# Dropping the padding of the stored head rows, and sharing out the last unit and the last layout

## The reference

```python
h = tok(x) ; h = concat([cls, h])                       # 128 x 17 x 256
h = h + attn(layernorm(h), wq, wk_a, wk_b, wv_a, wv_b, wo)
y = layernorm(h)
dist = softmax(mean(y @ Wr + br, axis=1))               # over 16 heads
idx = sort(top_k(dist, 4))                              # 4 heads of each image
Q, K, V = (y @ W + b, split into heads, gathered by idx, for W in Wq, Wk, Wv)
O = softmax(Q @ K.T / 8) @ V                            # 128 x 4 x 17 x 64
h = h + (O laid side by side, 17 x 256) @ Wo + bo
```

## Time and profile before

| | |
|---|---|
| runs | 415.77 us median of 3 (414.05 to 419.84) |
| the profiled execution | 419.29 us, span 417.0 us |
| mean granted TensorE clock | 0.844 of full speed |
| busy | PE 327.1 us (78%), PEld 264.0, DVE 253.6 (61%), ACT 200.6 (48%), POOL 170.6 (41%) |
| packets of the DMA queues | q1 (SP) 46944, q10 (ACT) 928, q0 (GpSimd) 576 |

### The profile page before, as it was taken

How to read it: one execution, slowest core, us unless ns; L and a number is a source line. 1 busy time by engine, 2 the same in 40 slices (tenths; PEclk the granted TensorE clock), 3 DMA queues, 4 the chain that set the end, 5 groups by cost and what they waited for, 6 DMA issues and landing times. The chain is left out here.

```text
span 417.0 us, 15363 instructions
## 1 busy us (share of the span) xinstructions
PE 327.1 (78%) x6575; PEld 264.0 (63%) x6575; DVE 253.6 (61%) x539; ACT 200.6 (48%) x453; POOL 170.6 (41%) x190
## 2 busy tenths in 40 slices
PE   1999999888977787757972588887978978562877
PEld 1896666435755566546851588877977877562466
DVE  2454354534678888875967387777766666441165
ACT  1113342544887766723890357666645656330240
POOL 3862000003366666630550824556673466424300
PEclk9999999999975555556995589999989999875889
DMA  7999000004400000000000779778787877822604
GB/s 214 398 422 404 29 2 0 0 0 153 151 5 4 6 6 3 5 3 4 2 1 0 232 221 301 225 225 221 216 247 222 244 208 217 243 46 60 211 27 191
DMA packets 48516, 55.98 MB, mean 134 GB/s; under 512 B 21536, under 2 KB 45248, under 8 KB 47936
## 3 DMA queue, kind: packets, MB, share of 16 engines
q1 hardware_dynamic: 46944, 52.54, 39.7%
q0 software_dynamic: 576, 2.23, 1.7%
q10 hardware_dynamic: 928, 0.23, 0.2%
HBM read 45.02 MB, written 9.96 MB: 132 GB/s over the span
## 5 line engine op out<-in xcount | busy, mean ns | idle before, releaser
L478 POOL TENSOR_TENSOR r<-r,cst 128x1088 f32<-128x1088 f32 x16 | 33.0, 2068 | 68.3 <-DVE ring L874 65.5
L1243 PE MATMUL ps<-r 128*128 128x256 f32 x192 | 46.1, 397 | 8.7 <-DMA r<-in_x 8.7
L1243 PEld LDWEIGHTS ps<-r 128*128 128x128 f32 x192 | 38.1, 201 | 17.5 <-issue 12.3
L1348 PE MATMUL ps<-r 17*32 17x34 f32 x2048 | 30.3, 242 | 17.2 <-DVE r L937 12.6
L1348 PEld LDWEIGHTS ps<-r 17*32 17x32 f32 x2048 | 27.1, 141 | 25.1 <-DVE r L937 19.5
L670 ACT ACTIVATE r<-r,cst 128x136 f32<-128x136 f32 x128 | 39.9, 399 | 0.0
L561 POOL TENSOR_TENSOR r<-r,quad 128x476 f16<-128x476 f16 x40 | 39.0, 1008 | 0.0
L1462 PE MATMUL ps<-r,ring 128*128 128x68 f16 x840 | 38.4, 203 | 0.0
L1460 PE MATMUL ps<-tile_head,wb 128*128 128x68 f16 x140 | 28.1, 201 | 12.8 <-DMA ring<-wsplit 11.1
L740 ACT ACTIVATE r<-ps 128x504 f16<-128x504 f32 (+1 forms) x50 | 32.0, 667 | 11.4 <-PE ps L1440 10.8
L1440 PE MATMUL ps<-pairs_of,r 128*128 128x56 f16 x680 | 30.4, 195 | 8.9 <-DVE r L1109 5.6
(11 more groups left out here) (158 smaller groups left out, 756.6 us busy)
## 6 DMA issues: line engine op xcount, KB each, us to landing
ring<-wsplit SPq DMA_DIRECT2D x140, 192.0 KB, 3.3
r<-in_x SPq DMA_DIRECT2D x3, 1536.0 KB, 15.8
padded_rows<-r SPq DMA_DIRECT2D x38, 112.0 KB, 3.0
r<-in_w SPq DMA_DIRECT2D x4, 768.0 KB, 12.1
wsplit<-ring SPq DMA_DIRECT2D x1, 3072.0 KB, 11.7
r<-in_x SPq DMA_DIRECT2D x4, 384.0 KB, 8.5
h<-in_pos SPq DMA_DIRECT2D x1, 1536.0 KB, 11.9
out<-h SPq DMA_DIRECT2D x3, 512.0 KB, 3.2
```

The lines of the kernel that those rows point to most:

```text
L478: pool.tensor_tensor(free(kx[:, u % 2, 0, :], (ROWH, UI), (NTOK, HH), (1, NTOK)), free(kr[:, 0, UI * NTOK * u:], (NTOK, UI), (0, HH), (1, ...
L1243: mm = pe.matmul(bank((n - 1) % 2, 0, D), xT[:, c, k, i * P:(i + 1) * P], tokw[:, k, :], start=k == 0, stop=k == PKT - 1)
L1348: mm = pe.matmul(bank(4 + 2 * (u % 2) + j // 2, at, at + 2 * NTOK)[QROW * c:QROW * c + QROW], v1[rows, UG * u + g, lo:lo + QROW], p1T[rows ...
```

## The change

Six things are altered. (1) `padded_rows` has a pitch of 17 rows a pair instead of 32, and each store takes 17 rows instead of 32. (2) The last unit is stored in halves: two times two transfers of seven tiles by SP and as many by ACT. (3) Of the last unit's block-diagonal matrices POOL makes those of half 0 and ACT those of half 1, in eight instructions of its own (one for each of four pairs, times two parts). (4) The product of the last half has PSUM bank 4, so it doesn't wait for DVE, and TensorE runs nine of the keep-awake matmuls before the last unit's products. DVE takes the last unit's score maxima before the second `head_out` of the unit before. (5) At the end POOL lays out slot 2 and the larger part of slot 3, DVE slot 0 and the first part of slot 3, ACT slot 1. (6) The ten turns go in the order `TURN_ORDER`, in which both halves alternate.

```diff
-PITCH = QROW * HD2
+PITCH = NTOK * HD2
...
-        def pair_rows_of(v, j):
-            return bass.AP(padded_rows.tensor, (v * PU + j) * PITCH, [(HD2, QROW), (IPG * PITCH, GU), (1, HD2)])
+        def pair_rows_of(v, j, lo=0, n=GU):
+            return bass.AP(padded_rows.tensor, (v * PU + IPG * lo + j) * PITCH,
+                           [(HD2, NTOK), (IPG * PITCH, n), (1, HD2)])
+        def stores(i):
+            return 16 * IPG * (len(range(i, NV, 2)) + (i == (NV - 1) % 2))
+        def weigh_bank(v, r):
+            return 4 if (v, r) == (NV - 1, 1) else 7
...
+        TURN_ORDER = [(0, 0), (0, 1), (1, 0), (0, 2), (1, 1), (0, 3), (1, 2), (0, 4), (1, 3), (1, 4)]
+        def laid_out(s, part):
+            lo, hi = (OG_FIRST, NTOK) if part else (0, OG_FIRST)
+            return (free(og2[:, lo, HD2 * s:], (D, hi - lo), (1, HD2)),
+                    free(og[:, s, HD2 * lo:], (HD2, hi - lo), (1, HD2)))
...
             def store_pairs(v, j):
-                sp.dma_start(pair_rows_of(v, j), o2[QROW * j:QROW * j + QROW, v % 2])\
+                sp.dma_start(pair_rows_of(v, j), o2[QROW * j:QROW * j + NTOK, v % 2])\
                     .then_inc(o2_stored[v % 2], 16)
...
-            for v in range(NV - 3, NV):
+            for v in range(NV - 3, NV - 1):
                 sp.wait_ge(o2_ready, 2 * (v + 1))
-                for j in range(IPG if v < NV - 1 else IPG // 2):
+                for j in range(IPG):
                     store_pairs(v, j)
+            for r in range(2):
+                sp.wait_ge(o2_ready, 2 * (NV - 1) + r + 1)
+                for j in range(IPG // 2):
+                    sp.dma_start(pair_rows_of(NV - 1, j, GR * r, GR),
+                                 o2[QROW * j:QROW * j + NTOK, (NV - 1) % 2, GR * r:GR * r + GR])\
+                        .then_inc(o2_stored[(NV - 1) % 2], 16)
...
-                    for r in range(2):
+                    for r in range(2 if v < NV else 1):
                         for x in range(2):
                             block_diagonal(v - 1, r, x)
...
+            for s, part in ((2, 0), (2, 1), (3, 1)):
+                pool.wait_ge(og_ready[s], 16)
+                dst, src = laid_out(s, part)
+                pool.tensor_copy(dst, src).then_inc(og2_pool, 1)
...
+            for x in range(2):
+                act.wait_ge(pT_low if x else pT_high, NV)
+                if x == 0:
+                    act.wait_ge(pv2_done, 2 * (NV - 2))
+                for i in range(IPG):
+                    nc.scalar.activation(free(bd[:, (NV - 1) % 2, x, GR, QROW * i:], (P, GR), (1, NTOK)),
+                                         free(p2Tx[:, (NV - 1) % 2, x, GR], (QROW, GR), (1, NTOK)), ACT.Copy,
+                                         scale=quad[:, i:i + 1]).then_inc(bd_last, 1)
...
-            dve.tensor_scalar(idx[:, :], at_slot, float(QROW), None, ALU.mult).then_inc(idx_ready, 1)
+            dve.tensor_scalar(idx[:, :], at_slot, float(NTOK), None, ALU.mult).then_inc(idx_ready, 1)
...
             def weigh2(v, r):
-                pe.wait_ge(bd_ready, 4 * v + 2 * r + 2)
+                last = (v, r) == (NV - 1, 1)
+                if last:
+                    pe.wait_ge(bd_last, 2 * IPG)
+                else:
+                    pe.wait_ge(bd_ready, 4 * v + 2 * r + 2)
...
-                if 2 * v + r >= 1:
+                if 2 * v + r >= 1 and not last:
                     pe.wait_ge(o2_ready, 2 * v + r)
...
+            keep_awake(9)
             weigh2(NV - 1, 0)
             weigh2(NV - 1, 1)
...
-            for i in range(len(BATCHES)):
-                turn_heads(0, i)
+            turn_heads(0, 0)
+            turn_heads(0, 1)
             turn_heads(1, 0)
             for i, batch in enumerate(BATCHES):
+                if i + 2 < len(BATCHES):
+                    turn_heads(0, i + 2)
                 if i + 1 < len(BATCHES):
                     turn_heads(1, i + 1)
```

More of the change, by code:

```diff
@@ L78, in build @@
     with ExitStack() as ctx:
-        padded_rows = nc.dram_tensor("padded_rows", (NPAIR * QROW, HD2), F32, kind="Internal").ap()
+        padded_rows = nc.dram_tensor("padded_rows", (NPAIR * NTOK, HD2), F32, kind="Internal").ap()
         wsplit = nc.dram_tensor("wsplit", (NE, P, WHEAD), F16, kind="Internal").ap()
@@ L204, in build @@
         bd_ready = sem("bd_ready")
+        bd_last = sem("bd_last")
         ps_clear = sem("ps_clear")
@@ L336, in turn_bank @@
         def turn_bank(k, i):
-            return i % 2 if k else i
+            return TURN_ORDER.index((k, i)) % 2
         def turned_heads(k, i, x):
@@ L580, in _ @@
             for i in range(2):
-                pool.wait_ge(o2_stored[i], len(range(i, NV, 2)) * IPG * 16)
+                pool.wait_ge(o2_stored[i], stores(i))
             pool.wait_ge(idx_ready, 1)
@@ L814, in _ @@
                                  scale=WS).then_inc(wo2_high, 1)
[L815 to L835, removed]
+            for r in range(2):
+                act.wait_ge(o2_ready, 2 * (NV - 1) + r + 1)
+                for j in range(IPG // 2, IPG):
+                    act.dma_start(pair_rows_of(NV - 1, j, GR * r, GR),
+                                  o2[QROW * j:QROW * j + NTOK, (NV - 1) % 2, GR * r:GR * r + GR])\
+                        .then_inc(o2_stored[(NV - 1) % 2], 16)
+            act.wait_ge(og_ready[1], 16)
+            for part in range(2):
+                dst, src = laid_out(1, part)
+                nc.scalar.activation(dst, src, ACT.Copy).then_inc(og2_act, 1)
+            for e, (k, i) in enumerate(TURN_ORDER):
+                act.wait_ge(og_turned, e + 1)
+                if k == 1 and i >= 2:
+                    act.wait_ge(wo2_done, BATCHES[i - 2][-1] + 1)
+                n = P * len(BATCHES[i])
+                nc.scalar.activation(turned_heads(k, i, 0), bank(turn_bank(k, i), 0, n), ACT.Copy, scale=XS)\
+                    .then_inc(ogT_high, 1)
         @block.vector
@@ L1201, in _, with lay_out @@
                                      op1=ALU.subtract).then_inc(wo2_split, 1)
-            def lay_out(s):
+            def lay_out(s, part):
                 dve.wait_ge(og_ready[s], 16)
-                for lo, hi in ((0, OG_FIRST), (OG_FIRST, NTOK)):
-                    dve.tensor_copy(free(og2[:, lo, HD2 * s:], (D, hi - lo), (1, HD2)),
-                                    free(og[:, s, HD2 * lo:], (HD2, hi - lo), (1, HD2))).then_inc(og2_dve, 1)
+                dst, src = laid_out(s, part)
+                dve.tensor_copy(dst, src).then_inc(og2_dve, 1)
             def low_heads(k, i):
-                e = len(BATCHES) * k + i
+                e = TURN_ORDER.index((k, i))
                 dve.wait_ge(ogT_high, e + 1)
@@ L1214, in low_heads @@
                     .then_inc(ogT_ready, 1)
-            lay_out(0)
+            lay_out(0, 0)
+            lay_out(0, 1)
             low_heads(0, 0)
+            lay_out(3, 0)
             low_heads(0, 1)
-            lay_out(2)
-            for i in range(2, len(BATCHES)):
-                low_heads(0, i)
             low_heads(1, 0)
             for i, batch in enumerate(BATCHES):
+                if i + 2 < len(BATCHES):
+                    low_heads(0, i + 2)
                 if i + 1 < len(BATCHES):
@@ L1508, in weigh2 @@
                     for m, (b, x) in enumerate(((0, 0), (0, 1), (1, 0))):
[L1509 removed]
+                        mm = pe.matmul(bank(weigh_bank(v, r), HD2 * i, HD2 * i + HD2), bd[:, v % 2, b, g, :], v2[:, v % 2, x, g, :],
                                        start=m == 0, stop=m == 2)
@@ L1545, in turn_heads @@
             def turn_heads(k, i):
[L1547 to L1550, removed]
-                    pe.wait_ge(ogT_ready, i + 1 if i < 2 else e - 1)
+                if k == 0:
+                    pe.wait_ge(og2_dve, 1 if i == 0 else 2)
+                    pe.wait_ge(og2_act, 1 if i == 0 else 2)
+                else:
+                    pe.wait_ge(og2_dve, 3)
+                    pe.wait_ge(og2_pool, 1 if i == 0 else 3)
+                e = TURN_ORDER.index((k, i))
+                if e >= 2:
+                    pe.wait_ge(ogT_ready, e - 1)
                 for at, n in enumerate(BATCHES[i]):
```

11 lines of the change are left out of this document (7 added, 4 removed).

## The result

The changed kernel takes 503.81 us (median of 4 runs, 503.39 to 504.37), the kernel before 414.91 (413.61 to 419.84): ratio 1.2125, 95% interval 1.207 to 1.218. The profiled execution took 504.23 us for a span of 502.4, 85.4 more than the profiled one of before, which lay above its median. Some executions of the kernel before are over 1.5% above its fastest; the medians behind the experiments, and the ratios, leave such executions out.

What follows compares the result with a forecast made beforehand. It took the one DMA engine receiving all 17-row stores as the bound: 267.1 + 50.4 weights + 173.3 stores + 1.6 + 5 = 497.4, plus 31.1 tail gives span 528.5, time 530.8, less 3.5: 527 us; range 480 to 600.

Steps and rivals of the forecast that it cites:

- One engine a store: Stores of 17 rows: each goes to one DMA engine, the same each time; stores land 111.5 us later; 75 in 100.
- even spread: Rival for 17-row stores: uneven shares over nine or more engines, so no change or small gain, 411 us; 12 in 100.
- engines in turn: Rival for 17-row stores: one engine each, but a different one in turn, 412 to 430, say 418 us; 5 in 100.
- the one with gaps: Rival for one-engine stores: each transfer starts only when the one before has ended, +70 us, 597 us; 7 in 100.
- The price of a piece: Stores: each 256 B piece takes 18.2 ns on its engine, so 9520 pieces take 173.3 us.
- the floor of 10.1 ns: Low bound on a 256 B store piece, from the rate of long loads: -77 us, 450 us; inside the forecast.
- the row at 20.5: High alternative for a 256 B store piece, 20.5 ns with two queues at once: +22 us, 549 us; inside the forecast.
- Does the engine ever run dry: Stage two's loop: SP's queue always has next entries, so the engine never idles; remaining weight loads add 50.4 us.
- The 3.5 us taken off at the end: Whole kernel: the earlier profiled execution lay 3.5 us above its median, so the forecast was lowered from 530.8 to 527 us.
- The signs: Changed profile: one completion packet a store, units of about 25 us, weight waits over 100 us, last stores near 497.
- The last unit: Last unit's edits: products ready by 463 under the store backlog, so worth nothing; without the backlog 2 to 3 us.
- The tail: After the last store: new layout copies and turn order change 0, bounds -1.5 and +2; 31.1 us stay.

Runs made afterwards that it cites:

- the 16 + 1 split: Changed kernel with each store cut into rows 0 to 15 per pair plus one transfer for row 16 of all four pairs: 414.4 us, ratio 1.000.

## Why the prediction was right, and which terms were off

**One engine a store: right.** The count of completion packets in the earlier trace rows gave two readings, equal shares or uneven ones; 17, 18, 19 and 25 rows on 1, 9, 1 and 5 engines, and 16 and 4 rows on 16 and 4, are what the rule of the divisor says. The Trainium skill's page "DMA: Bandwidth & Descriptors", section "Why a DMA increments its semaphore by 16 and not by 1", states this rule, and the trace agrees in all these counts. That it is the same engine each time is shown by the stores of one unit, which follow each other at 3.33 us instead of running side by side, and by the two queues that together move 18 GB/s. So the rivals of an even spread and of engines in turn fell, and the one with gaps fell too: the 18 GB/s go on from store to store.

**The price of a piece: too high.** I took 18.2 ns from the share of DMA time in the earlier trace rows. Durations overlap: the one engine starts a piece each 14.0 ns. Over 9520 pieces that is 133.3 instead of 173.3 us, -40. It was the largest miss, and the floor of 10.1 ns and the row at 20.5 lay on both sides.

**"Does the engine ever run dry": it does.** The prediction had SP running ahead, so that work other than stores cost 50.4 us, with 6.6 for start, landing and small packets; 5 of these 6.6 had no row behind them. From the first store at 267.71 to 470.34 are 202.6 us, less 133.3 are 69.3: +12.3 on those 57.0. By the packets the engine takes no store for 65.1 us between the first block of stores and the last, instead of the 50.4, while start and landing together are 3.1 and not 6.6; the pieces come to 1.2 more than at 14.0 ns. The step forgot that the issuing queue has only so much room. With one engine behind it SP is held at each store, issues the weights late, and then a register load of 1.4 to 3.1 us in each unit is in the open. Moving it gave 13.3 us back. With the first store 0.6 later the sum is 497.4 - 40.0 + 12.3 + 0.6 = 470.3, as measured.

**The 3.5 us taken off at the end: wrong here.** They stood for the distance of the profiled execution of before from its median. The four executions of the changed kernel lie within 1.0 us, the profiled one 0.4 above the median. So of the 23 us between 527 and 503.81 the pieces and the weights explain 27 down, and the tail, the end of the execution and this correction some 3.5 up. Two misses of opposite sign met, which is luck in part: with the price of a piece right and everything else as predicted the forecast would have been 487, near the lower end of its range.

**The signs: most came.** Completion packets were one a store, the units took 23.7 us on average for the 25 forecast, and one long wait came in each unit. The waits for weights over 100 us did not come: they were 67.6. The last three units have no weights behind their stores, and their delay shows as the 25.7 us at the end.

**The last unit: right.** The products were done at about 444.6, 25.7 us before the stores landed, so its edits were worth nothing here; the prediction had the products by 463 and the engine held by older stores till 480. Without the backlog they are worth 2.2 to 2.6 us by medians and 3.0 in the profile, for the 2 to 3 forecast.

**The tail: right within its bounds.** 32.1 instead of 31.1 us in the changed kernel, 0.4 in medians between the two tails on short stores: it is no gain. The stretch itself varies with the granted clock, whichever tail it has: the old tail took 29.1 us at 0.90 behind the 17-row stores alone and 31.1 at 0.88 before, the new one 29.1 at 0.90 in the kernel with the register load moved and 32.1 at 0.81 in the changed one.

**The even-spread rival's size.** It was put at 411 with the last unit's edits. The nearest thing measured is the 18-row store with nine equal shares and the same edits, 408.6 and 410.3 on two chips.

## What to carry to other kernels

Before cutting rows off a transfer, look at what the number of rows does to the number of DMA engines, and count completion packets in the profile to see it: 17 rows moved 47% fewer bytes than 32 and took 3.33 us of one engine instead of about half a microsecond of sixteen (four stores in 2.23 us). A row of padding that gives the count a larger divisor (18) costs 6% more bytes and keeps nine engines. And when one transfer is slow, count what stands behind it in its queue, since the queue that issues it is held too.

## What the runs showed that I had not expected

- Packets of 256 B from chip to device memory last 18 ns but start 14.0 ns apart on one engine, so shares of DMA time can stand above the work: 8.0% where one engine of 16 is 6.25%.
- SP's queue gets only a part of the way ahead of one engine: of a unit's four stores the first took 0.32 us to issue and the third and fourth 3.33 each, the time that the engine needs for one.
- Fewer pieces helped although the busiest engine had as many as before: nine engines with 28 pieces each instead of sixteen with 28 took the median from 415.9 to 410.7 us, and in another group from 415.3 to 408.3. TensorE's waits for weights were 4.3 and 6.7 us in the two profiles instead of 11.1. Why the 16 + 1 split, with still less on the busiest engine, gave no such gain stays open: its ratio is 1.000 (0.994 to 1.006), while 18 rows with the same other edits had 0.989 and 0.978. TensorE's waits for weights were 7.2 us in its profile, so these waits alone don't decide it.
